# Summing attention's exponentials over key tiles on GpSimd before the product with ones, and the values product ahead of it

## The reference

```python
q, k, v = heads of layernorm(x) @ Wqkv
scores = where(causal, q @ k.T * 32 ** -0.5, -1e9)
x = x + (softmax(scores) @ v) @ Wo
g = silu(layernorm(x) @ w1q.T) * (layernorm(x) @ w3q.T)
x = x + g @ w2q.T
```

## Time and profile before

| | |
|---|---|
| median of 3 runs | 727.8 us (727.48 to 729.08) |
| the profiled execution, first to last instruction | 727.0 us |
| PE busy | 630.4 us (87%) |
| DVE busy | 436.0 us (60%) |
| ACT busy | 335.2 us (46%) |
| POOL busy | 136.4 us (19%), 205 instructions |
| product with ones, L1102 to `sum_bank` | 43.3 us, group of 512 instructions by 484 ns (partly beside each other) |
| `affine_select`, L558 | 96, 45.4 us |
| reciprocal, L844 | 16, 53.7 us, 3.36 us each |

### The profile page before, as it was taken

One profiled execution on the slowest core, in us unless ns is written; L12 is line 12 of the kernel. 1 busy time (PEld: TensorE's weight loads), 2 busy tenths in 40 slices (PEclk: granted clock), 3 DMA queues, 4 the chain that ended last, 5 costly groups with the idle time before them and its releaser, 6 DMA issues.

```text
span 727.0 us, 10700 instructions
## 1 busy us (share of the span) xinstructions
PE 630.4 (87%) x3892; PEld 300.6 (41%) x3892; DVE 436.0 (60%) x816; ACT 335.2 (46%) x551; POOL 136.4 (19%) x205
## 2 busy tenths in 40 slices
PE   2695687677988999999979999999979999997998
PEld 1142333333444444444444444444434544443443
DVE  7767767974655668634575777535556775244431
ACT  2556756852345585511456555501557645202330
POOL 2000012311100233410001225401002233211330
PEclk9997888667999999999999999999999999997999
DMA  8061121300020000011100000021000000120001
GB/s 330 16 227 58 48 79 54 116 1 1 1 73 16 16 16 1 1 59 60 52 23 17 16 16 1 1 76 40 15 16 16 1 16 1 44 72 1 0 1 59
DMA packets 13930, 30.22 MB, mean 42 GB/s; under 512 B 2442, under 2 KB 2442, under 8 KB 13876
## 3 DMA queue, kind: packets, MB, share of 16 engines
q1 hardware_dynamic: 13876, 29.50, 12.8%
HBM read 20.97 MB, written 4.19 MB: 35 GB/s over the span
## 4 chain that ended last, share of the span: by engine, by line
PE 64%; DVE 17%; ACT 11%; issue 5%; DMA 2%; SPq 0%; POOL 0%; DVEq 0%; ACTq 0%; POOLq 0%
PE work L999 25%; PE work L1139 11%; PE work L1030 10%; PE sum_bank L1102 6%; PE o_bank L1102 4%; PE prob_bank L1083 3%; PE score_bank L1056 3%; ACT k_stack L625 3%; DVE block_max L829 3%; ACT probs L642 2%; DVE inv_sum L844 1%; ACT late L684 1%; DMA late<-in_L_ffn_w 1%; ACT late L657 1%; ACT q_stack L625 1%
## 5 line engine op out<-in xcount | busy, mean ns | idle before, releaser
L999 PE MATMUL work<-late,w_ternary 128*128 128x512 f16 (+1 forms) x704 | 168.3, 390 | 9.6 <-DVE late L864 8.1
L829 DVE TENSOR_REDUCE block_max<-score_bank 128x4 f32<-128x512 f32 x160 | 102.8, 684 | 52.3 <-PE score_bank L1058 52.2
L999 PEld LDWEIGHTS work<-late,w_ternary 128*128 128x128 f16 (+1 forms) x704 | 69.9, 102 | 90.6 <-DVE late L864 14.2
L642 ACT ACTIVATE probs<-prob_bank,scalars 128x512 f32<-128x512 f32 x160 | 100.6, 681 | 7.0 <-PE prob_bank L1083 6.0
L568 POOL TENSOR_TENSOR late<-late 128x512 f16<-128x512 f32 (+1 forms) x44 | 51.0, 1159 | 208.5 <-ACT late L663 208.5
L1139 PE MATMUL work<-w_ternary,late 128*128 128x512 f16 (+1 forms) x352 | 77.2, 379 | 0.0
L864 DVE SCALAR_TENSOR_TENSOR late<-late,work 128x512 f32<-128x512 f32 (+1 forms) x44 | 30.3, 688 | 68.7 <-ACT late L657 68.4
L1056 PE MATMUL score_bank<-k_stack,q_stack 96*128 96x512 f16 (+3 forms) x256 | 62.7, 310 | 9.3 <-DVE block_max L829 8.4
L844 DVE RECIPROCAL inv_sum<-sum_bank 128x512 f32<-128x512 f32 x16 | 53.7, 3358 | 21.5 <-PE sum_bank L1102 21.5
L1030 PE MATMUL work<-xt_hi,wqkv_hi 128*128 128x512 f16 x128 | 51.5, 402 | 17.0 <-DVE wqkv_lo L778 10.4
L647 ACT ACTIVATE ot_hi<-o_sb 128x512 f16<-128x512 f32 x16 | 10.1, 630 | 121.0 <-DVE o_sb L850 121.0
(11 more groups left out here) (104 smaller groups left out, 911.3 us busy)
## 6 DMA issues: line engine op xcount, KB each, us to landing
late<-in_L_ffn_w SPq DMA_DIRECT2D x6, 768.0 KB, 6.5
x_res<-in_L_attn_x SPq DMA_DIRECT2D x16, 256.0 KB, 2.7
out_y<-x_res SPq DMA_DIRECT2D x16, 256.0 KB, 2.0
late<-in_L_attn_Wqkv SPq DMA_DIRECT2D x4, 768.0 KB, 8.9
xn<-in_L_attn_x SPq DMA_DIRECT2D x3, 1024.0 KB, 5.3
late<-in_L_ffn_w SPq DMA_DIRECT2D x4, 682.5 KB, 3.9
q_stack<-q_stack SPq DMA_DIRECT2D x16, 128.0 KB, 2.3
k_stack<-k_stack SPq DMA_DIRECT2D x16, 128.0 KB, 2.3
```

Source lines behind the costliest of these rows:

```text
L642: act.activation(probs[:, u, :], prob_bank[u % 2][:], ACT.Exp, scale=scalar(exp_scale)).then_inc(prob_free, 1)
L829: dve.tensor_reduce(block_max[:, u, :], score_bank[u % 2][:].rearrange("p (k c) -> p k c", c=P), AX_X, ALU.max).then_inc(score_free, 1)
L999: last = pe.matmul(bank, lhs, rhs, start=(n == 0), stop=(n == len(terms) - 1))
```

## The change

GpSimd adds the exponentials of the key tiles per pair of heads, after the selects, into a new tile `added` of 4 x 384 columns: queries 128 to 511 of key tiles 0 and 1 (768 columns for the pair), plus key tile 2 (512), plus key tile 3 (256). The product with ones then runs over 128 columns of `probs` (queries 0 to 127, which only key tile 0 has) and 384 of `added` per head, 512 in place of 1280. The values product goes first, and a wait for `added_done` stands between it and the sums. Nothing else is changed: DVE still starts with the reciprocal.

```diff
+        added = sb("added", [P, HG, S - P], F32)
...
                     pool.affine_select(out=view, in_=view, compare_op=ALU.is_ge, fill=0.0, base=0,
                                        pattern=[[0, n], [1, P]], channel_multiplier=-1).then_inc(selected, 1)
+
+                pool.wait_ge(selected, count(ps.att, SELECTS * GROUPS, SELECTS * g + 3 * (pairs[p] + 1)))
+                n = ADDS * g + 3 * pairs[p]
+                sums = added[:, 2 * pairs[p]:2 * pairs[p] + 2, :]
+                pool.tensor_tensor(sums, probs[:, u:u + 4:3, P:S], probs[:, u + 1:u + 5:3, 0:S - P],
+                                   ALU.add).then_inc(added_done, 1)
+                pool.wait_ge(added_done, count(ps.att, ADDS * GROUPS, n + 1))
+                pool.tensor_tensor(sums[:, :, P:3 * P], sums[:, :, P:3 * P],
+                                   probs[:, u + 2, :].rearrange("p (h c) -> p h c", h=2), ALU.add).then_inc(added_done, 1)
+                pool.wait_ge(added_done, count(ps.att, ADDS * GROUPS, n + 2))
+                pool.tensor_tensor(sums[:, :, 2 * P:3 * P], sums[:, :, 2 * P:3 * P],
+                                   probs[:, u + 1:u + 5:3, S - P:S], ALU.add).then_inc(added_done, 1)
...
-                for bank, full in ((sum_bank, sums_full), (o_bank, values_full)):
-                    for kt in range(ST):
-                        for h in range(HG):
...
-                            lhs = ones[:] if bank is sum_bank else v_sb[:, kt, col:col + HD]
-                            last = pe.matmul(bank[HD * h:HD * (h + 1), S - n:S], lhs, probs[:, u, off:off + n],
-                                             start=(kt == 0), stop=(kt == ST - 1), skip_group_check=True)
-                    last.then_inc(full, 1)
+                for kt in range(ST):
+                    for h in range(HG):
...
+                        last = pe.matmul(o_bank[HD * h:HD * (h + 1), S - n:S], v_sb[:, kt, col:col + HD],
+                                         probs[:, u, off:off + n], start=(kt == 0), stop=(kt == ST - 1),
+                                         skip_group_check=True)
+                last.then_inc(values_full, 1)
+                pe.wait_ge(added_done, count(ps.att, ADDS * GROUPS, ADDS * (g + 1)))
+                for cols in (slice(0, P), slice(P, S)):
+                    for h in range(HG):
+                        src = probs[:, 5 * (h // 2) + 3 * (h % 2), cols] if cols.start == 0 else added[:, h, :]
+                        last = pe.matmul(sum_bank[HD * h:HD * (h + 1), cols], ones[:], src,
+                                         start=True, stop=True, skip_group_check=True)
+                last.then_inc(sums_full, 1)
```

More of the change, by code:

```diff
@@ L61 @@
 SELECTS = 6
+ADDS = 6
 WEIGHTS = ("w1", "w3", "w2")
@@ L397, in build @@
         selected = sem("selected")
+        added_done = sem("added_done")
         sums_full = sem("sums_full")
@@ L1094, in values @@
                     pe.wait_ge(o_ready, count(ps.att, GROUPS, g))
-                for bank, full in ((sum_bank, sums_full), (o_bank, values_full)):
-                    for kt in range(ST):
-                        for h in range(HG):
-                            u, off, n = [(u, off, n) for u in range(NU) for hh, tile, off, n in UNITS[u]
-                                         if (hh, tile) == (h, ST - 1 - kt)][0]
-                            col = (g * HG + h) * HD
-                            lhs = ones[:] if bank is sum_bank else v_sb[:, kt, col:col + HD]
-                            last = pe.matmul(bank[HD * h:HD * (h + 1), S - n:S], lhs, probs[:, u, off:off + n],
-                                             start=(kt == 0), stop=(kt == ST - 1), skip_group_check=True)
-                    last.then_inc(full, 1)
+                for kt in range(ST):
+                    for h in range(HG):
+                        u, off, n = [(u, off, n) for u in range(NU) for hh, tile, off, n in UNITS[u]
+                                     if (hh, tile) == (h, ST - 1 - kt)][0]
+                        col = (g * HG + h) * HD
+                        last = pe.matmul(o_bank[HD * h:HD * (h + 1), S - n:S], v_sb[:, kt, col:col + HD],
[9 more added lines that the diff above has]
+                last.then_inc(sums_full, 1)
             def project(ps, step):
```

## The result

The changed kernel takes 757.55 us (median of 4 runs, 754.0 to 759.2), the kernel before 728.02 us beside it: a ratio of 1.0391, 95% interval 1.036 to 1.0421. The change costs 29.5 us. The forecast, slower at 748.3 us, had the sign and most of the mechanism and was 9 us short; the median lies 0.6 us above the range's upper end, and inside it if the ratio is applied to the 727.8 us that the forecast started from (756.3). On the profiled executions, on which the forecast's parts were summed, the loss is 28.2 us (727.0 to 755.2) where 20.5 was forecast: 7.7 short.

A forecast was written before the change was run, and what follows sets the result against it. Loop balanced between TensorE and the path sums, reciprocal, `o_sb`, `block_max`/`ot_hi`, exponentials. First pass 10.5 + middle passes 7.2 + last attention 2.8 = 20.5 us on 727.0: 747.5, plus 0.8 for the median: 748.3 us; range 738 to 757.

The forecast's parts named there:

- TensorE's work: 512 columns in place of 1280 in the product with ones: 1.30 us less per group, 20.8 us over 16 groups.
- The adds: GpSimd's three adds per pair of heads: 3 x 1.16 = 3.48 us, with two semaphore waits 3.6 us.
- Middle pass: Each of two middle passes: groups 0 to 2 late by 1.0, 1.7, 2.2 us, group 3 gains 1.3; loses 3.6.
- The port: Rival, 17%: GpSimd's adds and DVE's copies into k_stack exclude each other; 5 us, 2 to 3 in first pass; 756.
- The last attention: Last attention pass, without variance powers in GpSimd's queue: group 2 loses 1.4 us, the pass 2.8.
- Were the adds free: Middle pass, group 0, if the adds cost nothing: reciprocal 0.9 us later, group about even.
- First pass: Reciprocal 7.5 us late in group 1, 2.9 in group 3 with group 2's 0.8 included; together 10.5 us.
- the reload: First pass, GpSimd: code reloaded between all-reduce and `tensor_tensor`, 6.79 us idle, now between selects and adds of group 1.
- The "against": Objection to the shared-port rival: DVE's copies that get in between two adds cost nothing.
- Reload cheap: Rival, 14%: the 6.79 us may hold waiting that isn't a reload; first pass loses about 3 us, time 741.
- slack on DVE: Rival, 4%: DVE's path has more slack, one group's lateness made up before the next; even, 728 to 730.
- TensorE the bound: Rival, 5%, faster: TensorE bounds the loop, each group of three passes gives up to 1.3 us; 715.

The follow-up runs named there:

- run 1: Three kernels without adds: values first with 1280-column sums, 754.27 us; values first with 512-column sums of key tile 0, 733.18; those short sums ahead of values, 706.71.
- run 6: Against the changed kernel: the change only in group 3 of the three later attention passes; 723.14 us, 0.9947 of the kernel before; again 722.55 us, 0.9941.
- run 4: Against the changed kernel: the three all-reduces of the FFN weights' magnitudes replaced by small additions on GpSimd; 755.39 us, 1.0388 of the kernel before.
- run 5: Against the kernel before: only the first pair's adds, in groups 0 and 1 of the three later passes, used by nothing; 730.72 us, ratio 1.0054.
- run 8: Against the changed kernel: the wait for the adds and the short sums placed ahead of the values product; 779.35 us, 1.0718 of the kernel before.
- run 7: Adds and short sums in group 3 of the later passes, plus short sums for group 2's first pair, ahead of values; 726.17 us, 0.9982 of before.

## Why the prediction was right or wrong

- *TensorE's work, 20.8 us in 16 groups:* right. Run 1 gives 20 to 21 us; group 3 of run 6 saves 1.28 us.
- *The adds, 3.6 us per pair:* too little. They take 1.81 + 1.26 + 0.73 = 3.80 us, and 4.04 from the end of the selects to their own (group 1 above: 276.55 + 1.35 = 277.90 to 281.21 + 0.73 = 281.94). Writing f32, 512 columns took 1.26 us where the subtraction that writes f16 took 1.17, and each start cost some 0.08 us beyond.
- *Middle pass 3.6 us, measured 7.0 and 5.6:* the mechanism, group by group, is as forecast; the sizes are not. In the second middle pass, which has no more of the low clock than before, the step `values` starts 0.4 us too late in group 0 and 0.6 in group 1, before its own terms have done anything. That is TensorE's longer wait for `late` behind DVE's copies (0.97 and 1.05 us, before 0.49): the port, which the sum put at nothing. From the start of `values` to the reciprocal it is then 1.63 and 1.68 us more than before, and 1.6 and 1.7 were forecast, so in these two groups the longer adds cost nothing on top. They cost in group 2, where two sets stand in GpSimd's queue: 1.0 us over the forecast 2.2. That makes 3.6 into 5.6. The first middle pass has 1.4 more from the clock that fell behind the stand of 1.92 us. The last attention lost 4.6 where 2.8 was forecast, 1.8 over by the same two terms.
- *"Were the adds free, about even":* right for groups 0 and 1 of run 1's kernel with short sums (in the first middle pass its reciprocals are 1.8, 2.1 and 3.1 us later than before in groups 0, 1 and 2, of which 0.95 came from the first pass); group 2 lost 1.0.
- *First pass 10.5 us, measured 12.0:* the idle time between selects and adds was 6.93 us (6.8 forecast), the reciprocal of group 1 6.8 us late (7.5). In group 3 the values started when forecast (177.27, forecast 169.6 + 7.5) but ran at the low clock, 4.50 us and not 3.13; that is the missing 1.4. Run 4 corrects the reading. The forecast hung nearly all of the term on the reload, and its rival gave 3 us for a pass without it; without it the pass still lost 9.3. That the size came out near is in part luck.
- *The port (17%):* not the other way it could go but an addition to the forecast, and smaller than the rival's 5 us for groups 0 and 1: 2.3 us by the trace of run 5, some 1.0 us in the second middle pass of the changed kernel. The "against" was wrong: one copy gets through behind each add, and together they still lose 2.3 us. In the first pass run 4 points to the port in place of the reload; what it alone costs there no run shows.
- *Reload cheap (14%), slack on DVE (4%), TensorE the bound (5%):* refuted by the 6.93 us, by the milestones and by the 20.2 us that TensorE stands for `block_max`.

On the profiled executions the forecast was 7.7 us short. Four terms were mis-sized or left out: the first pass by 1.5 us (the low clock in group 3); the port and the longer adds by 2.0, 2.0 and 1.8 us in the three later attentions; the low clock in the first middle pass, 1.4 us. That is 8.7 us. Against it stands a gain nobody forecast, 1.7 us of clock ahead of the last attention, and 0.7 us were lost in the last FFN, which I have not traced: 7.7 in all. What stays open is how the first pass divides between reload, order and port.

## What to carry to other kernels

Ask first what the next engine waits for: an operation put ahead of the reciprocal costs its whole length even where TensorE gains by it, and the order alone took 27 us here where the shorter product gave 21. Offload where the list already has cover (group 3: 0.994 of before); half of group 2, the one other place tried alone, lost most of that gain again (0.998). When work goes to an idle engine, price its length with the same types, the port it shares with DVE, and the slow stretch of TensorE's clock that may follow a new stand: here it followed one of three stands of 1.92 us, and in run 8 all nine of 3 us or more for `added`.

## What the runs showed of the hardware

- TensorE's granted clock was 0.50 (1.2 GHz) for about 3.4 us behind single stands of 1.92 us (kernel after, 294.9) and 3.05 us (run 8), where it had been 1.00 before and during them. It stayed at 1.00 behind two equal stands of 1.92 us in the same execution (458.96 and 619.49). I had expected this only in the first pass, with its long idle stretches.
- A `tensor_tensor` on GpSimd that follows an all-reduce came 6.91 and 6.93 us after the work before it, with selects in between, and the selects themselves came at once. With the all-reduces replaced (run 4) the same adds followed the selects at once.
- GpSimd's add took 1.81, 1.26 and 0.73 us for 768, 512 and 256 columns with an f32 output; the subtraction with an f16 output took 1.17 us for 512. No run separates the type from the shape.
- DVE's f16 copies of 32 x 512, 0.29 us each, took 1.07, 1.33 and 0.79 us beside GpSimd's three adds (run 5): one copy got through behind each add.
- A product in four strips of 32 rows, two with 1280 columns and two with 512, took 2.17 us, as with 1280 in all four (run 7).
